# Two layers of graph attention on one core: a block's residual and moments in layer 1 placed two granule slots later, its averaging in two slots

## What is computed

```python
def layer0(h, adj, a):                      # layer 1 of the title
    e = (h @ a[:64])[:, None] + (h @ a[64:])[None, :]
    e = where(e > 0, e, 0.01 * e)
    e = where(adj > 0, e, -9e15)
    return softmax(e, axis=1) @ h
def layer1(x, adj, w, a, bias):             # layer 2
    wh = x @ w
    e = leaky_relu((wh @ a[:64])[:, None] + (wh @ a[64:])[None, :], 0.01)
    return softmax(where(adj > 0, e, -1e9), axis=1) @ wh + bias
x = layernorm(x + layer0(x, adj, a0))
x = layernorm(x + layer1(x, adj, w, a1, bias))
```

## Time and profile before

| | us |
|---|---|
| median of 3 runs | 491.33 |
| lowest and highest | 489.75, 494.29 |
| the profiled execution | 490.02 |
| its span | 487.6 |

### The profile page before, as it was taken

One profiled execution on the slowest core, in us unless ns is written; L12 is line 12 of the kernel. 1 busy time (PEld: TensorE's weight loads), 2 busy tenths in 40 slices (PEclk: granted clock), 3 DMA queues, 4 the chain that ended last, 5 costly groups with the idle time before them and its releaser, 6 DMA issues.

```text
span 487.6 us, 11722 instructions
## 1 busy us (share of the span) xinstructions
PE 435.6 (89%) x4409; PEld 411.8 (84%) x4409; DVE 413.6 (85%) x751; ACT 394.3 (81%) x586; POOL 85.3 (18%) x59
## 2 busy tenths in 40 slices
PE   0799858998988989899998997989999999999993
PEld 0379757987988889899888986989999999999993
DVE  3789998889989898989989997999677786967776
ACT  2685188778897888779889918999999999999940
POOL 0012221512415133151431210001010010101011
PEclk9987979997999979889898988999999999999998
DMA  7999999999999999999994300152130303021100
GB/s 184 255 245 273 273 269 276 330 310 313 326 320 328 308 311 307 311 335 303 321 322 143 130 1 0 58 162 64 36 97 0 97 0 97 11 86 55 42 12 13
DMA packets 83525, 89.27 MB, mean 183 GB/s; under 512 B 7426, under 2 KB 79394, under 8 KB 83490
## 3 DMA queue, kind: packets, MB, share of 16 engines
q1 hardware_dynamic: 48834, 54.57, 39.8%
q10 hardware_dynamic: 34656, 34.21, 25.5%
HBM read 79.32 MB, written 9.45 MB: 182 GB/s over the span
## 4 chain that ended last, share of the span: by engine, by line
PE 42%; DVE 24%; DMA 18%; issue 12%; ACTq 1%; ACT 1%; SPq 1%; POOL 0%; POOLq 0%; DVEq 0%
PE acc L467 40%; DMA stage<-in_adj 17%; DVE narrow L872 5%; DVE turned L884 4%; DVE pos L893 2%; DVE num L987 1%; DMA kept<-in_x 1%; DVE num L994 1%; DVE red L982 1%; DVE kept L794 1%; DVE bn L999 1%; DVE num L984 1%; DVE kept L884 1%; PE flip L393 1%; DVE kept L788 1%
## 5 line engine op out<-in xcount | busy, mean ns | idle before, releaser
L602 ACT ACTIVATE neg<-srow,dcol 128x512 int8<-128x512 f32 (+1 forms) x320 | 222.5, 861 | 11.8 <-issue 8.0
L467 PE MATMUL acc<-xy_old,pos 128*128 128x195 bf16 x1024 | 195.9, 261 | 18.1 <-POOL pos L1143 11.4
L467 PE MATMUL acc<-xy_old,neg 128*128 128x195 bf16 x1024 | 195.7, 261 | 0.0
L467 PE MATMUL acc<-stage,pos 128*128 128x195 bf16 x1024 | 180.6, 250 | 2.6 <-issue 2.6
L467 PE MATMUL acc<-stage,neg 128*128 128x195 bf16 x1024 | 180.5, 250 | 0.0
L602 ACT ACTIVATE neg<-xy_old,dcol 128x512 int8 (+1 forms) x192 | 137.5, 1034 | 0.0
L467 PEld LDWEIGHTS acc<-xy_old,pos 128*128 128x128 fp8e4 x1024 | 106.5, 104 | 26.9 <-issue 25.4
L467 PEld LDWEIGHTS acc<-xy_old,neg 128*128 128x128 fp8e4 x1024 | 105.8, 103 | 1.4
L467 PEld LDWEIGHTS acc<-stage,pos 128*128 128x128 fp8e4 x1024 | 101.7, 99 | 3.4 <-issue 3.0
L467 PEld LDWEIGHTS acc<-stage,neg 128*128 128x128 fp8e4 x1024 | 101.2, 99 | 0.3
L872 DVE TENSOR_SCALAR narrow<-stage 128x4096 uint8<-128x4096 int32 x32 | 74.3, 2320 | 13.1 <-DMA stage<-in_adj 12.2
(11 more groups left out here) (134 smaller groups left out, 345.9 us busy)
## 6 DMA issues: line engine op xcount, KB each, us to landing
stage<-in_adj ACTq DMA_DIRECT2D x64, 512.0 KB, 9.3
stage<-in_adj SPq DMA_DIRECT2D x64, 512.0 KB, 9.2
spill<-turned SPq DMA_DIRECT2D x16, 512.0 KB, 7.7
turned<-spill SPq DMA_DIRECT2D x16, 512.0 KB, 3.7
xy_old<-score_rows SPq DMA_DIRECT2D x6, 256.0 KB, 4.4
out<-x1s SPq DMA_DIRECT2D x7, 128.0 KB, 1.9
xn<-in_x SPq DMA_DIRECT2D x1, 768.0 KB, 16.6
kept<-in_x SPq DMA_DIRECT2D x4, 128.0 KB, 3.9
```

Source lines behind the costliest of these rows:

```text
L467: last = nc.tensor.matmul(acc[:, r, c * XW:(c + 1) * XW], masks[c][:, t // BYTES, t % BYTES, r * P:(r + 1) * P], xy[layer][:, g * GT + t, ...
L602: last = nc.scalar.activation(o[:, t // BYTES, t % BYTES, :], row, ACT.Sign, bias=dcol[:, layer, col:col + 1])
```

## The change

`average` is split: it keeps the weighting (L982), and the new `quotient` holds the rest. In layer 1 they stand in two slots: `average(0, s)` in slot 2, `quotient(0, s)` in slot 3. `residual_sum` and `moments` of a block go from slot 3 of its own body into slot 0 of the next one; those of block 6 stand after the loop, ahead of the last mask. `normalize` of block s - 1 on ACT then follows the signs and the load of granule 1 in body s. `turn_x1` on PE goes behind granule 0, `project` behind granule 1. POOL does all four `positive` of a block before `inverse_std`. The small steps for layer 2's shift go one body or one or two slots later. Layer 2 itself keeps its order.

```diff
@@ PE, body0
                 granule(0, s, NG - 1)
                 if last:
-                    pe.wait_ge(shift_ready, 3)
-                if not first:
-                    turn_x1(s - 1)
-                if last:
+                    spread_max(0)
                     score_row(1, 0)
                 else:
                     score_row(0, s + 2)
...
                 granule(0, s + 1, 0)
+                if last:
+                    pe.wait_ge(shift_ready, 3)
                 if first:
                     source_vectors()
                 else:
+                    turn_x1(s - 1)
+                granule(0, s + 1, 1)
+                if not first:
                     project(s - 1)
+                granule(0, s + 1, 2)
                 if s == NS - 3:
                     pe.wait_ge(xT_ready, NS + s)
                     turn_max(0)
-                granule(0, s + 1, 1)
-                if s == NS - 3:
-                    spread_max(0)
-                granule(0, s + 1, 2)
@@ ACT, body0
                     load_next(s + 1, g)
                     if first and g == 1:
                         copy_weights()
+                    if g == 1 and not first:
+                        normalize(s - 1)
                 signs(0, s + 2, 0)
                 load_next(s + 2, 0)
                 if not first:
                     copy_wh(s - 1)
-                normalize(s)
@@ DVE, average
                 link(layer, s, 1, V.tensor_tensor(red[:, part, :, :], red[:, part, :, :], factors, ALU.mult), part)
+
+            def quotient(layer, s, part=every):
+
                 dve.wait_ge(x1_ready, layer * NS + s + 1)
@@ DVE, body0
-                for g in range(NG):
-                    to_bytes(s + 1, g)
-                    if g == 0 and s == NS - 2:
-                        near_shift()
-                    if g == 0:
-                        mask0(s, NG - 1)
-                    if g == 2:
-                        average(0, s)
-                    if g == 0 and s == NS - 3:
-                        far_columns(0)
-                    if g == 3 and s == NS - 3:
-                        column_max(0)
-                    if g == 3:
-                        residual_sum(0, s)
-                    if g:
-                        mask0(s + 1, g - 1)
-                    turn(s + 1, g)
-                    if g == 1:
-                        read_acc(0, s)
-                    if g == 2 and s == 0:
-                        source_vectors()
-                    if g == 3:
-                        moments(0, s)
+                to_bytes(s + 1, 0)
+                mask0(s, NG - 1)
+                turn(s + 1, 0)
+                if s > 0:
+                    residual_sum(0, s - 1)
+                    moments(0, s - 1)
+                to_bytes(s + 1, 1)
+                if s == NS - 2:
+                    column_max(0)
+                mask0(s + 1, 0)
+                turn(s + 1, 1)
+                read_acc(0, s)
+                to_bytes(s + 1, 2)
+                if s == NS - 3:
+                    far_columns(0)
+                if s == NS - 2:
+                    near_shift()
+                average(0, s)
+                mask0(s + 1, 1)
+                turn(s + 1, 2)
+                if s == 0:
+                    source_vectors()
+                to_bytes(s + 1, 3)
+                quotient(0, s)
+                mask0(s + 1, 2)
+                turn(s + 1, 3)
...
             for s in range(NS - 1):
                 body0(s)
+            residual_sum(0, NS - 2)
+            moments(0, NS - 2)
             last_mask0()
@@ POOL
             with pool.Fori(0, NS - 2) as s:
-                for g in range(NG - 1):
+                for g in range(NG):
                     positive(s + 1, g)
                 inverse_std(0, s)
-                positive(s + 1, 3)
```

More of the change, by code:

```diff
@@ L666, in _ @@
                     load_next(NS - 1, g)
+                if g == 1:
+                    normalize(NS - 3)
             copy_wh(NS - 3)
@@ L1073, in _ @@
             average(0, NS - 1)
+            quotient(0, NS - 1)
             residual_sum(0, NS - 1)
@@ L1098, in _ @@
             average(1, 0)
+            quotient(1, 0)
             residual_sum(1, 0)
@@ L1111, in _ @@
                         average(1, s)
+                        quotient(1, s)
                         residual_sum(1, s)
@@ L1118, in _ @@
                 average(1, NS - 1, part)
+                quotient(1, NS - 1, part)
                 residual_sum(1, NS - 1, part)
```

## The result

| | before | after |
|---|---|---|
| median, us (16 runs each) | 490.68 | 494.09 |
| lowest and highest | 488.51, 495.44 | 491.62, 495.75 |
| the profiled execution | 490.02 | 494.77 |
| its span | 487.6 | 492.8 |

The account below looks back on a forecast made before the run. No engine alone bound it: in each block the chain ran through a load of adjacency words, otherwise DVE. DVE's 11.0 us of load waits less 6 x 0.9 gave 5.6: 490.02 - 5.6 = 484.4, stated as 485, range 480 to 491.

Parts of the forecast that it names:

- The end of the layer: Layer 1's last products on PE: mask 1.4 us sooner, projection up to 2.1 us between granules; net taken as nothing.
- 0.7 more: Upper edge of the net delay of PE's last products in layer 1; the lower edge was 1.4 us less.
- PE: ... same work, priced at nothing in the block: PE's turn_x1 behind granule 0 and project behind granule 1 cost nothing, since PE waits for masks there.
- Cost on the path: nothing: ACT's normalize, two slots later, may wait for POOL; signs behind it are wanted over 7 us later, so no cost.
- Two waits a block of 0.35 us and 0.2 for slot 2: DVE's remaining load waits: 0.35 us each ahead of slots 3 and 0, 0.2 at slot 2; 0.9 a block.
- none ahead of slot 1: Expected sign in the profile after: DVE waits about 5 us for loads in sum, none of it ahead of slot 1.
- The windows: Time from a load's issue to the narrow wanting it, two slots less 3.04 us; narrowest grows from 9.45 to 10.18.
- the two extra microseconds of slot 0 in the last block and the two saved at the end of the first cancel: DVE's work moved into slot 0 costs two microseconds in the last block, saves two in the first: net nothing.
- Can the transfers go faster at all?: Loop transfers: 9.44 MB a block at 345 GB/s takes 27.4 us, just under DVE's 27.88, so little room.
- DVE alone: Rival, the loop: all of DVE's load waits go, 11.0 us gained, 480.3 us; chance 0.16.
- The transfers are as fast as they get: Rival, the loop: throughput stays near 317 GB/s, waits only move to slots 3 and 0; gain 2.0, 489 us; chance 0.28.
- ACT issues the upper half late: Rival, the loop: ACT's copy waits for PE's turned rows, delaying its load; up to 9 us slower, 500 us; chance 0.09.

Follow-up runs that it names:

- e1: The changed kernel, with ACT's copy of block 5's projection moved behind the first four signs of layer 2's granule 1: 488.32 us, 0.9952 of before.
- e5: The changed kernel, with PE's projection of block 5 ahead of granule 1 again in the last body alone: 489.02 us, 0.9963 of before.
- e12: The kernel before, with only PE's projection of block 5 moved behind granule 1 in the last body: 498.35 us, 1.0157 of before.
- e11: The kernel before with the split alone, quotient in slot 3 ahead of the residual sum: 489.49 us, 0.9978 of before.
- e10: The changed kernel without the split, quotient back in slot 2: 498.01 us, 1.0161 of before.
- e2: The changed kernel, with DVE's narrowing converting only half of each load's words, all loads kept (result wrong): 481.06 us, one execution.
- e3: The changed kernel, with 512 KB loads cut in pieces of 2 KB instead of 1 KB (result wrong): 488.44 us, one execution.
- e4: The changed kernel, with only an eighth of each spill and its reload moved (layer 2 uses stale bytes): 484.88 us, one execution.
- e9: The changed kernel, block 5's projection ahead of granule 1 in the last body, ACT copying block 6's turned rows three signs sooner: 489.00 us, 0.9957 of before.
- e7: The kernel before, with 512 KB loads cut in pieces of 2 KB instead of 1 KB (result wrong): 486.18 us, one execution.

## Why the prediction was wrong

**The end of the layer** is the step that failed for the time. Its arithmetic on PE held term by term: from slot 2's `narrow` the mask came 1.40 us sooner (257.61 - 254.33 = 3.28, where before it was 259.65 - 254.97 = 4.68), and the projection between the granules took 2.03. Together that is 0.6 later, the edge "0.7 more". That the last product still came 1.40 sooner is 0.64 from the loop, and for the rest luck with the clock. In before PE had its lower clock level for 3.4 us of granule 1 of the last block (columns as in the earlier trace rows); in after it had not, and that granule took 5.69 us instead of 7.13:

```profile
264.40:267.80 3.40, 3.40 (x24) 3.16 (x22) 3.33 (x7) 3.40 (x7) 0.00 (x0) 0.51 0.21 77
```

But I stopped at the last product. The two sentences that hid the loss are "PE: ... same work, priced at nothing in the block" and "Cost on the path: nothing" for ACT: I asked who waits behind `normalize`, in a block of the loop, and never asked who waits behind ACT's copy of what `project` makes. In the loop that copy has signs behind it that DVE wants late. In the last body it has the rest of layer 1's epilogue behind it, in one list. Price measured: 5.06 us of pause and 1.42 of a slower granule, less the 1.40 gained ahead: 5.1 net. e1 and e5 take the added wait away and the loss with it, e12 makes both alone.

**Two waits a block of 0.35 us and 0.2 for slot 2** was mis-sized. I forecast 0.9 us of DVE's wait a block, about 5 in sum; it is 11.5 (8.9 to 11.5 in the five kernels with this loop). The slots are nearly right (7.73, 7.10, 6.13, 7.15 against 7.48, 7.18, 6.13, 7.09), and slot 2's wait did go. But "none ahead of slot 1" is wrong (0.66 in the block shown). The windows did tell where the waits stand: before, ahead of slots 1 and 2 (9.79 and 9.45 us), after, mostly ahead of slots 0 and 3, now the narrowest (10.18 and 10.27), in e11 ahead of slots 2 and 3 (4.1 and 5.7 us of wait), in e10 ahead of slots 0 and 1 (5.3 and 2.8). They did not tell how long they are in sum: 11.0, 11.5, 10.8 and 9.6 us. What I had wrong is the flight: I held flights of 10.2 and 11.50 us, taken from before, against the new windows as if they were a fixed length. The seven on the chain of after from 69 us on take 10.64 to 14.42, 12.66 on average. Three of them land ahead of slot 1, 12.91, 12.83 and 13.30 us long (issued at 146.41, 175.75 and 205.00), though its window had grown to 11.53. And "the two extra microseconds of slot 0 in the last block and the two saved at the end of the first cancel" failed: the saving in the first body went into the wait of 2.67, the cost in the last one stayed.

**"Can the transfers go faster at all?"** took 345 GB/s from the best slices and so 27.4 us a block. With DVE mostly early they hold 332, 28.6 us (e2). The same row has slices of 364, 380, 385 and 416 GB/s, so it is not so that no slice reaches what the rival *DVE alone* wants; but the block as a whole stays at 323. DVE without any wait needs 28.1 (the four slots above: 7.73 + 7.10 + 6.13 + 7.15). Two limits half a microsecond apart, and the block takes 29.7, one more than the larger. e3's larger pieces and e4's fewer bytes bring that one microsecond back. That it is the two halves of `stage` that couple the limits is argued: no run has a third.

**The rivals.** *The transfers are as fast as they get* was right on the loop: 319 GB/s, waits moved to other slots, a gain of 2.27 us over five blocks, where its sum had 2.0 over six. One piece of evidence for it was misread: the block from 211.14 took 29.77 without any wait for a load, since DVE waited in it for ACT (the row at 216.14 above) and had small steps for the shift. No run changed the size of a transfer, which this rival went by; e3 and e7 changed the rate with all of them at 512 KB. Its 489 is what e1, e5 and e9 measure once the seam is mended (488.3 to 489.0). *DVE alone is the bound* fell: no loop with all the bytes in pieces of 1 KB came near 27.88 us a block. *ACT issues the upper half late* did not happen: the copy of the turned rows begins 5.08 us into slot 2 (200.78), against my 4.9 for its input, it waits 1.29 for PE there, but the load behind it is issued with SP's (204.48 on ACT, 204.46 on SP), and over the whole run loads take a median of 9.5 and 9.1 us on the two queues, as before (9.3 and 9.2). Nor does a granule at the lower clock level cost the 3.4 us that I gave it: it took 7.13 and 7.18 us (before, e12) against 5.69. The time did land where this rival had it, over 491.5, but by another way: the right engine and the right kind of wait, ACT standing for PE in order, at the wrong place.

**What stays open.** Why pieces of 1 KB flow at 317 to 332 GB/s, in memory or in the engines, was not separated. In e1 the profiled execution begins its 128 products at 324.03, as the one of before does, while the medians are 2.8 us apart; the runs of one kernel spread over up to 7 us, and no profile here says which stretch differs between runs. Part of what separates the profiles of e1 and after is such a difference: the 1.51 us of an earlier last product come from a loop that is the same in both.

## What to carry to other kernels

When a step on one engine moves behind a larger one, list for each reader of its result what stands behind that reader in its own in-order list, and do it again for the last turn of the loop, where what stands behind is not the loop's next turn but the start of the next stage. A matrix engine that gets to such a seam sooner gains nothing if the seam's input comes from another engine's list. Before expecting a balance of slots to pay, take the rate of the transfers from a kernel in which their consumer is mostly early, not from the best slices of one in which it isn't.

## What the runs showed of the hardware

A longer pause of PE cost twice: its own length, and more time at the lower clock level behind it. After 3.97 us between products (before) PE had its lower clock level for 3.4 us and the 64 products of the next granule took 6.99; after 9.03 us it had it for 10.2 us and they took 8.41; at the full clock they take 5.70. The pause of 4.80 in e5 has 3.4 us, that of 5.62 in e1 6.8, those of 9.2 in e10 and e12 10.2; after 3.65 in e11 the next granule runs at the full clock (5.70). Around the short pause ahead of layer 2's granule 1 there is another stretch at the lower clock in each of these kernels. The pause alone doesn't settle it: ahead of the second granule of the last block of layer 1 PE stood idle for 1.33 us before and had the lower level for 3.4 us behind it, while after it stood idle for 2.03 us and kept the full clock. The Trainium skill (TensorE: Matmul & The Clock Gate, section What's actually happening) has the clock follow how busy PE was just before. The trace agrees for the long pauses (4.01 us idle in 9.03, then 10.2 us at the lower level), but in before the clock also fell after a pause of 3.97 us in which PE was busy for 3.70.

The DMA share of a stretch stayed at 1.05 to 1.10 in every loop, from 302 to 333 GB/s, with DVE waiting nearly 29 us for loads or under 4. I read it as saying that packets were in flight throughout, not how fast they went.
